# State-space scan: a third of the products with the C row moved to GpSimd, the other states left in PSUM

## What is computed

```python
delta = jax.nn.softplus(dt_raw @ W_dt + b_dt)          # [tokens, 256]
A = -jnp.exp(A_log)                                    # [256, 16]
dA = jnp.exp(delta[..., None] * A)
dBx = delta[..., None] * Bp[:, :, None, :] * xv[..., None]
_, h = jax.lax.associative_scan(comb, (dA, dBx), axis=1)   # h = dA * h_before + dBx
y = jnp.einsum('bldn,bln->bld', h, Cp)                 # sum over the 16 states
y = y + xv * D
```

## Time and profile before

| | us |
|---|---|
| median of 3 runs | 3803.92 (3802.51 to 3805.05) |
| the profiled execution, device time | 3794.94 |
| its span in the profile | 3793.2 |
| VectorE busy in the span | 2935.6 (77%) |
| GpSimd busy in the span | 594.6 (16%) |
| the scan, from its first scan instruction to the end of its last product with C | 1580.66 to 1808.55 |

### The profile page before, as it was taken

One profiled execution on the slowest core, in us unless ns is written; L12 is line 12 of the kernel. 1 busy time (PEld: TensorE's weight loads), 2 busy tenths in 40 slices (PEclk: granted clock), 3 DMA queues, 4 the chain that ended last, 5 costly groups with the idle time before them and its releaser, 6 DMA issues. The chain is left out here.

```text
span 3793.2 us, 127348 instructions
## 1 busy us (share of the span) xinstructions
PE 3169.5 (84%) x54136; PEld 2068.2 (55%) x54136; DVE 2935.6 (77%) x3631; ACT 2527.9 (67%) x4874; POOL 594.6 (16%) x1629
## 2 busy tenths in 40 slices
PE   2999999659998798555587589999999999999538
PEld 1666666425555576122345356666666666666424
DVE  5999999538885212799547499999999999999553
ACT  1899999527778343433123179999999999999522
POOL 0000001023211000266000011111111111111210
PEclk7999999859999899799788689999999999999759
DMA  4000000130000000342018755555555555555310
GB/s 121 9 8 9 8 10 6 42 78 12 12 7 3 18 17 15 131 148 78 6 45 233 193 123 123 134 119 130 125 128 128 120 133 120 135 121 131 92 30 11
DMA packets 190763, 295.10 MB, mean 78 GB/s; under 512 B 87922, under 2 KB 119994, under 8 KB 189142
## 3 DMA queue, kind: packets, MB, share of 16 engines
q1 hardware_dynamic: 185238, 275.64, 28.5%
q10 hardware_dynamic: 2608, 6.37, 0.8%
q0 software_dynamic: 2352, 4.99, 0.5%
HBM read 224.83 MB, written 53.35 MB: 73 GB/s over the span
## 5 line engine op out<-in xcount | busy, mean ns | idle before, releaser
L889 ACT ACTIVATE channels_qk<-psum 128x512 f32<-128x512 f32 x3842 | 2060.3, 595 | 257.4 <-PE psum L718 221.3
L957 DVE TENSOR_REDUCE l2f_chunk_max<-psum 128x2 f32<-128x1024 f32 x1144 | 1323.5, 1217 | 79.3 <-PE psum L694 72.8
L957 DVE TENSOR_REDUCE chunk_max<-psum 128x2 f32<-128x1024 f32 (+2 forms) x832 | 916.3, 1156 | 100.4 <-PE psum L694 55.3
L694 PE MATMUL psum<-l2f_k_parts,l2f_q_parts 48*128 48x512 bf16 x2288 | 696.8, 388 | 42.0 <-DVE l2f_chunk_max L957 31.0
L718 PE MATMUL psum<-l2f_q_parts,l2f_k_parts 51*128 51x128 bf16 x8968 | 706.1, 217 | 3.6 <-issue 3.6
L736 PE MATMUL psum<-channels_qk,l2f_v_and_ones 128*9 128x128 f32 x17920 | 698.4, 274 | 12.1 <-issue 11.1
L694 PE MATMUL psum<-k_parts,q_parts 48*128 48x512 bf16 (+3 forms) x1664 | 427.6, 384 | 101.8 <-DMA q_parts<-q_rows_dram 70.6
L718 PEld LDWEIGHTS psum<-l2f_q_parts,l2f_k_parts 51*128 51x128 bf16 x8968 | 482.1, 94 | 34.8 <-ACT channels_qk L889 25.9
L736 PE MATMUL psum<-channels_qk,v_and_ones 128*9 128x128 f32 x12544 | 494.2, 276 | 0.9 <-ACT channels_qk L889 0.5
L718 PE MATMUL psum<-q_parts,k_parts 51*128 51x128 bf16 x6272 | 433.3, 219 | 32.8 <-DMA q_parts<-minus_max_rows 12.1
L736 PEld LDWEIGHTS psum<-channels_qk,l2f_v_and_ones 128*9 128x9 f32 x17920 | 386.2, 90 | 119.3 <-issue 24.1
(11 more groups left out here) (488 smaller groups left out, 3126.1 us busy)
## 6 DMA issues: line engine op xcount, KB each, us to landing
l2f_k_parts<-l2f_k_parts_dram SPq DMA_DIRECT2D x588, 192.0 KB, 3.7
l2f_v_and_ones<-expert_v_dram SPq DMA_DIRECT2D x144, 288.0 KB
l1a_bc_rows<-ssm_rows_dram SPq DMA_DIRECT2D x32, 512.0 KB, 4.6
expert_v_dram<-l2f_v_and_ones SPq DMA_DIRECT2D x8, 1152.0 KB, 9.4
channels_qk<-ssm_rows_dram SPq DMA_DIRECT2D x16, 512.0 KB
l2f_q_parts<-l2f_gathered_q_parts SPq DMA_DIRECT2D x444, 16.0 KB
k_parts<-k_rows_dram ACTq DMA_DIRECT2D x32, 192.0 KB, 7.0
q_parts<-q_rows_dram SPq DMA_DIRECT2D x64, 96.0 KB, 2.5
```

What stands on the lines that cost most here:

```text
L694: last = nc.tensor.matmul(c.ps[:, 2 * (n % 2) + j, 0:width], at.q[64 * j:64 * j + ROWS, tile % SLOTS, pair, :], kx(tile)[64 * j:64 * j + R ...
L889: nc.scalar.activation(at.prob[:, s % 4, j, 0:kts, :].rearrange("p k q -> p (k q)"), c.ps[:, ring.bank(i, n), 0:kts * 2 * P], ACT.Exp, sca ...
L957: v.tensor_reduce(at.mx[:, 4 * g + 2 * pp:4 * g + 2 * pp + 2, chunk], c.ps[:, 2 * (n % 2):2 * (n % 2) + 2, 0:span.width(tile, chunk)], X, ...
```

## The change

The product with the C row of step 2, 5, 8, ... 62 (21 of the 64 steps) goes to GpSimd, which issues it behind its product with B of two steps later. Its scan still writes into `u` in SBUF. In the other 43 steps the scan writes its states over the decay, in PSUM, and VectorE's product with C reads them from there. `hc_ready` becomes two semaphores, one for each engine that writes `hc`. GpSimd's product with B no longer waits for the product with C of two steps ago; it waits for the scan of four steps ago (whose buffer it takes), for the carry and, where that step was GpSimd's, for its product with C. ScalarE, before it writes a decay, waits also for VectorE's product with C of two steps ago, and for the copy of the carry, which now comes ahead of the decay.

```diff
@@ -1633,8 +1633,23 @@
         hc = c.sb(sctx, "state_c", [P, U, TH], F32)
         carry = c.sb(sctx, "carry", [P, S], F32)
         diag = c.sb(sctx, "d_diagonal", [P, 2, P], F32)
-        da_ready, u_ready, scanned, hc_ready, added, diag_ready, carried, y_copied = (c.sem("s_" + n) for n in (
-            "da_ready", "u_ready", "scanned", "hc_ready", "added", "diag_ready", "carried", "y_copied"))
+        da_ready, u_ready, scanned, added, diag_ready, carried, y_copied = (c.sem("s_" + n) for n in (
+            "da_ready", "u_ready", "scanned", "added", "diag_ready", "carried", "y_copied"))
+        hc_by_vector, hc_by_pool = c.sem("s_hc_by_vector"), c.sem("s_hc_by_pool")
+
+        def on_pool(step):
+            return step % 3 == 2
+
+        def wait_state_c(eng, step):
+
+            of_pool = sum(on_pool(k) for k in range(step + 1))
+            if on_pool(step):
+                eng.wait_ge(hc_by_pool, of_pool)
+            else:
+                eng.wait_ge(hc_by_vector, step + 1 - of_pool)
+
+        def state(step):
+            return u[:, step % U, :] if on_pool(step) else decay(step)
 
         def tokens(step):
             return slice(step // S * TH, (step // S + 1) * TH)
@@ -1648,7 +1663,8 @@
                 for m in range(2, AHEAD):
                     rows.load(sp, m)
                 for m in range(AHEAD, S):
-                    sp.wait_ge(hc_ready, 2 * (m - AHEAD) + 2)
+                    for step in (2 * (m - AHEAD), 2 * (m - AHEAD) + 1):
+                        wait_state_c(sp, step)
                     rows.load(sp, m)
 
             @block.scalar
@@ -1657,9 +1673,12 @@
                     h, n = step % 2, step % S // 2
                     if step >= 2:
                         act.wait_ge(scanned, step - 1)
+                        if not on_pool(step - 2):
+                            wait_state_c(act, step - 2)
+                    if 2 <= step < S + 2:
+                        nc.scalar.activation(carry[:, step - 2:step - 1], state(step - 2)[:, TH - 1:TH], ACT.Copy).then_inc(carried, 1)
+                        act.wait_ge(carried, step - 1)
                     nc.scalar.activation(decay(step), delta[:, h, tokens(step)], ACT.Exp, scale=a[:, h, n:n + 1]).then_inc(da_ready, 1)
-                    if 2 <= step < S + 2:
-                        nc.scalar.activation(carry[:, step - 2:step - 1], u[:, (step - 2) % U, TH - 1:TH], ACT.Copy).then_inc(carried, 1)
                     if step == S + 2:
                         act.wait_ge(added, S)
                         for g in range(2):
@@ -1667,13 +1686,26 @@
 
             @block.gpsimd
             def _(pool):
+                def times_c(step):
+                    _, c_row = rows.wait(pool, step // 2)
+                    pool.wait_ge(scanned, step + 1)
+                    if step >= U:
+                        pool.wait_ge(added, step - U + 1)
+                    nc.gpsimd.tensor_tensor(hc[:, step % U, :], u[:, step % U, :], c_row, ALU.mult).then_inc(hc_by_pool, 1)
+
                 for step in range(2 * S):
                     b_row, _ = rows.wait(pool, step // 2)
-                    if step >= 2:
-                        pool.wait_ge(hc_ready, step - 1)
                     if step >= U:
+                        pool.wait_ge(scanned, step - U + 1)
                         pool.wait_ge(carried, min(step - U + 1, S))
+                        if on_pool(step - U):
+                            wait_state_c(pool, step - U)
                     nc.gpsimd.tensor_tensor(u[:, step % U, :], dx[:, step % 2, tokens(step)], b_row, ALU.mult).then_inc(u_ready, 1)
+                    if step >= 2 and on_pool(step - 2):
+                        times_c(step - 2)
+                for step in (2 * S - 2, 2 * S - 1):
+                    if on_pool(step):
+                        times_c(step)
 
             @block.vector
             def _(dve):
@@ -1682,16 +1714,17 @@
                     v.tensor_scalar(diag[:, h, :], c.ident[:, :], dvec[:, h:h + 1], None, ALU.mult).then_inc(diag_ready, 1)
                 for step in range(2 * S):
                     _, c_row = rows.wait(dve, step // 2)
-                    if step == S:
-                        dve.wait_ge(carried, S)
+                    if step >= S:
+                        dve.wait_ge(carried, step - S + 1)
                     dve.wait_ge(da_ready, step + 1)
                     dve.wait_ge(u_ready, step + 1)
-                    v.tensor_tensor_scan(u[:, step % U, :], decay(step), u[:, step % U, :],
+                    v.tensor_tensor_scan(state(step), decay(step), u[:, step % U, :],
                                          0.0 if step < S else carry[:, step - S:step - S + 1], ALU.mult, ALU.add).then_inc(scanned, 1)
-                    dve.wait_ge(scanned, step + 1)
-                    if step >= U:
-                        dve.wait_ge(added, step - U + 1)
-                    v.tensor_tensor(hc[:, step % U, :], u[:, step % U, :], c_row, ALU.mult).then_inc(hc_ready, 1)
+                    if not on_pool(step):
+                        dve.wait_ge(scanned, step + 1)
+                        if step >= U:
+                            dve.wait_ge(added, step - U + 1)
+                        v.tensor_tensor(hc[:, step % U, :], state(step), c_row, ALU.mult).then_inc(hc_by_vector, 1)
 
             @block.tensor
             def _(pe):
@@ -1704,7 +1737,7 @@
                             for b in range(2):
                                 nc.tensor.matmul(ps[:, 2 * h + b, :], diag[:, h, :], xv[:, h, step // S * TH + b * 512:step // S * TH + (b + 1) * 512],
                                                  start=True, stop=False)
-                    pe.wait_ge(hc_ready, step + 1)
+                    wait_state_c(pe, step)
                     for b in range(2):
                         last = nc.tensor.matmul(ps[:, 2 * (step % 2) + b, :], c.ident[:, :], hc[:, step % U, b * 512:(b + 1) * 512],
                                                 start=False, stop=step % S >= S - 2)
```

## The result

The changed kernel took 3769.68 us (median of 4 runs, 3766.18 to 3772.7) against 3804.49 us of the kernel before beside it: a ratio of 0.9902, with a 95% interval of 0.9883 to 0.9921. It is 34.8 us faster.

The account below looks back on a forecast made before the run. VectorE was taken to bound the scan. Scan 227.9 - 198.8 = 29.1 us, less 1.4 for hand-overs and 0.8 at the end, gives 26.9; 3803.9 - 26.9 = 3777.0 us, range 3771.0 to 3790.0.

Parts of the forecast that it names:

- VectorE bounds, and is held by GpSimd only with two SBUF operands: In the scan VectorE never stands still; GpSimd holds it when both operands are in SBUF, not when one is in PSUM.
- 3.46 and 3.53 us for a step with its product: VectorE, first and second half of the tokens: scan of 2.31 or 2.38 plus product with C of 1.15 us.
- 2.28 and 2.34 us for a step without product: VectorE, the 21 steps whose product goes to GpSimd: each costs its scan alone, 10 at 2.28, 11 at 2.34.
- GpSimd, 85 x 2.346, level with VectorE, and 1.4 us of hand-overs: GpSimd's 85 products back to back take 9.38 us per three steps, VectorE 9.20 or 9.40; mutual waits cost 1.4 us.
- The 2.3 us that GpSimd would wait for the third scan: At the start GpSimd fills the ring with five products, then waits for scan 2 and loses 2.3 us.
- The tail, 0.8 us: At the end TensorE takes steps 62 and 63 late, behind GpSimd's last product; costs 0.8 us.
- The PSUM operand at no cost: VectorE's 43 products reading PSUM: nothing taken, bounds -0.4 to +1.3 us in all; the skill's rule would give some 2.8 us.
- Waits on GpSimd: Rival: each of GpSimd's 85 products has 0.14 us ahead of it, 12 us in all, time 3787; chance 0.16.
- Still held, PSUM or not: Rival: GpSimd still holds VectorE's 43 products with C, 11.7 us for three steps, 21 us slower, 3825; chance 0.06.
- A second pass over the bank: Rival: scan in place in PSUM collides reading and writing, 43 x 1.07 = 46 us on VectorE, 3822; chance 0.05.
- the fixed 0.06 us: Bound for the scan writing PSUM: a fixed 0.06 us would be 2.6 us in all.
- The ring: Rival: TensorE's order or the ring of hc stalls VectorE once in three steps, 25 us, gain gone, 3802; chance 0.04.

## Why the prediction was right, and where it failed

- *VectorE bounds, and is held by GpSimd only with two SBUF operands.* Right, shown from both sides: products of 1.22 us from PSUM whatever GpSimd does, up to 3.37 us from SBUF.
- *3.46 and 3.53 us for a step with its product.* Right (1592.26 - 1588.80 = 3.46 in the first half), as the 223.7 us without GpSimd show.
- *2.28 and 2.34 us for a step without product.* Here a term was mis-sized. I took the length of the scan's record, though for the product I had taken start to start, and had put the 0.08 us overlap only among the bounds. Start to start it is 2.19 and 2.26: 10 x 0.09 + 11 x 0.08 = 1.8 us too dear.
- *GpSimd, 85 x 2.346, level with VectorE, and 1.4 us of hand-overs.* The same fault: back to back a product takes 2.31. Three steps cost GpSimd 9.23 us and VectorE 9.10 or 9.29, the ring of four takes up the difference, and no scan waited. The 2.3 us that GpSimd would wait for the third scan came as 2.4. The hand-overs cost nothing.
- *The tail, 0.8 us.* 0.7.
- With these, 26.9 + 1.8 + 1.4 + 0.1 = 30.2, against 30.4 in the profile, and the forecast would have been 3773.7. The mechanism was right; in the sum, the steps without product and the hand-overs were mis-sized by 3.2 us. The other 4 us down to the measured 3769.68 are not in the scan.
- *The range.* This is the step that failed outright. Its lower end had the smaller terms of the scan in it and still lay above the median, because it allowed only 1.4 us for what lies outside the scan, the spread of three runs. The profiles of the two kernels show 12 us there, and the medians of the changed kernel beside those of before differ by 34.8 to 39.4 us. A range for a median of a few runs had to reach some 5 us further on both sides. Why the difference outside mostly favours the changed kernel is open.
- *The PSUM operand at no cost.* Right: 1225 ns, against 1226 from SBUF. By the rule of the Trainium skill (VectorE: DVE Perf Modes, "The TRN2 errata") it would have been 65 ns more, an estimate from that page; no run agrees with that.
- *The rivals.* Waits on GpSimd: it would have shown gaps of 0.14 ahead of every product, but the products follow each other every 2.31 us. Still held, PSUM or not: it did not happen from PSUM (1225 ns); with SBUF operands it does, at about what was worked out (11.35 us for three steps against 11.7). A second pass over the bank: 2281 against 2278 ns, which leaves no room for the fixed 0.06 us among the bounds either; no run shows that term. The ring: VectorE never waited for TensorE.

## What to carry to other kernels

Where GpSimd and VectorE both work on SBUF, look for VectorE instructions that end only when GpSimd's beside them do. Here one operand in PSUM freed both, and only with it did moving work to GpSimd pay. Work out a stream of instructions from start to start, not from the lengths of the records, which overlap here by some 0.03 to 0.16 us. And where the change sits in 6% of the span, compare that stretch in the profiles: it repeats to 0.1 us, where the whole varies by 12.

## What was not expected of the hardware

The hold works both ways: in the variant with SBUF states GpSimd's three products took 8.94 us instead of 6.99.

TensorE's granted clock fell in the scan. Here are the windows of 190 us inside it (the third number from the end is the granted clock, as a share), first of a profile of the kernel before, then of the changed one:

```profile
1590.00:1780.00 190.00, 111.93 (x224) 39.22 (x222) 188.12 (x108) 65.12 (x86) 125.46 (x54) 0.98 0.42 147
```

```profile
1590.00:1780.00 190.00, 138.47 (x259) 54.19 (x257) 188.59 (x104) 75.95 (x95) 185.99 (x81) 0.88 0.44 152
```

Of the two levels, 1.2 and 2.4 GHz, it was granted the upper one nearly throughout before (0.98), with additions every 3.56 us. Now TensorE waits up to 4.5 us for GpSimd's product with two more steps queued behind it, and then works them off in one go; it was at the lower level for part of the time (0.88). In the same window the variant with no product on GpSimd has 0.98, and the variants with every fourth and every second have 0.91 and 0.92: the fall comes with the products on GpSimd, not with the states in PSUM. The additions took 686 ns in the mean instead of 616. That cost nothing, since no wait of VectorE's or GpSimd's in the scan is ended by TensorE.
